# Attention in groups of three heads, four groups in flight, with the experts' weights split inside it

## The reference

```python
def _sot(q):
    qn = q / (norm(q) + 1e-08)
    C = where(eye, 1000.0, 1.0 - einsum('bhnd,bhmd->bhnm', qn, qn))
    log_K, log_v = -C / 0.1, 0
    for _ in range(10):
        log_u = log_marg - logsumexp(log_K + log_v[..., None, :], axis=-1)
        log_v = log_marg - logsumexp(log_K + log_u[..., :, None], axis=-2)
    z = exp(log_u[..., :, None] + log_K + log_v[..., None, :])
    return where(eye, 1.0, z / max(z))
attn = softmax(_sot(q) * 16 ** -0.5)
out = einsum('bhnm,bhmd->bhnd', attn, v)
...
for e in range(8):
    mid = relu(einsum('bsd,fd->bsf', x, W1[e]) + b1[e])
    out = out + w[..., e:e + 1] * (einsum('bsf,df->bsd', mid, W2[e]) + b2[e])
```

## Time and profile before

| | |
|---|---|
| median of 3 runs | 5091.24 us (5083.55 to 5093.23) |
| the profiled execution | 5082.8 us, of which its span 5081.0 us |
| embed and project | 0 to 1203 us |
| attention | 1209 to 3991 us |
| the weights (`prepare`) | 3994 to 4057 us |
| router, experts, combine | 4060 to 5081 us |
| ScalarE busy, whole span | 60% |
| matmuls of `multiply` (L653) | 58368 |

### The profile page before, as it was taken

One profiled execution on the slowest core, in us unless ns is written; L12 is line 12 of the kernel. 1 busy time (PEld: TensorE's weight loads), 2 busy tenths in 40 slices (PEclk: granted clock), 3 DMA queues, 4 the chain that ended last, 5 costly groups with the idle time before them and its releaser, 6 DMA issues. The chain is left out here.

```text
span 5081.0 us, 191812 instructions
## 1 busy us (share of the span) xinstructions
PE 4568.4 (90%) x84561; PEld 3640.2 (72%) x84562; DVE 3744.7 (74%) x8549; ACT 3051.0 (60%) x4474; POOL 310.8 (6%) x349
## 2 busy tenths in 40 slices
PE   5999999885999999999999999999999278599990
PEld 4777777642788888888888888888888144377770
DVE  8999999743577777777777777777777644355557
ACT  4777777633566666666666666666664234377771
POOL 0000000000000000000000000000000014433330
PEclk9999999986999999999999999999999576699995
DMA  1000000032000000000000000000000222322214
GB/s 63 33 35 27 27 27 27 29 98 66 14 16 17 22 16 16 22 17 16 16 23 16 16 21 17 16 16 23 16 12 9 92 89 97 112 69 67 71 60 152
DMA packets 164003, 203.02 MB, mean 40 GB/s; under 512 B 66736, under 2 KB 141744, under 8 KB 160752
## 3 DMA queue, kind: packets, MB, share of 16 engines
q1 hardware_dynamic: 149680, 159.86, 10.5%
q0 software_dynamic: 13632, 32.66, 1.8%
HBM read 123.64 MB, written 68.81 MB: 38 GB/s over the span
## 5 line engine op out<-in xcount | busy, mean ns | idle before, releaser
L653 PE MATMUL y_ps<-k_sb,x_sb 128*12 128x256 f16 x58368 | 1683.4, 273 | 13.3 <-DVE x_sb L890 13.0
L653 PEld LDWEIGHTS y_ps<-k_sb,x_sb 128*12 128x12 bf16 x58368 | 1425.6, 88 | 186.9 <-issue 24.4
L772 ACT ACTIVATE y_sb<-y_ps 128x256 f32<-128x256 f32 x912 | 348.3, 382 | 841.8 <-PE y_ps L653 841.8
L781 ACT ACTIVATE k_new<-cos,k_bias 128x512 f32<-128x512 f32 x768 | 520.9, 683 | 171.2 <-PE cos L680 171.2
L663 PEld LDWEIGHTS turned_x<-rows_in,y_sb 128*128 128x128 f32 x3648 | 477.7, 191 | 118.3 <-issue 71.6
L921 DVE CUSTOM_DVE_ANT_0 plan<-plan,u_rows,v_last 128x512 f32<-128x512 f32 x768 | 535.2, 744 | 4.3 <-issue 0.3
L663 PE MATMUL turned_x<-rows_in,y_sb 128*128 128x16 f32 x3648 | 526.6, 258 | 8.4 <-ACT y_sb L772 8.2
L256 PE MATMUL acc<-w_hl,feat_h 128*128 128x384 f16 x2688 | 454.6, 327 | 87.5 <-ACT feat_h L241 87.5
L795 ACT ACTIVATE plan<-plan,p_bias,p_scale 128x1024 f32<-128x1024 f32 x384 | 464.2, 1238 | 9.7 <-DVE p_scale L932 9.7
L909 DVE TENSOR_TENSOR plan<-k_sb 128x1024 f32<-128x1024 f16 x384 | 459.3, 1217 | 0.0
L936 DVE TENSOR_TENSOR k_sb<-k_new,k_sb 128x2048 f16<-128x2048 f32 x192 | 436.1, 2272 | 30.4 <-ACT k_sb L789 30.4
(11 more groups left out here) (256 smaller groups left out, 7199.3 us busy)
## 6 DMA issues: line engine op xcount, KB each, us to landing
x_in_sb<-expert_rows SPq DMA_DIRECT2D x39, 528.0 KB, 3.7
xt<-in_x_dram SPq DMA_DIRECT2D x16, 1280.0 KB, 5.9
q_left<-q_parts SPq DMA_DIRECT2D x192, 64.0 KB, 3.0
q_right<-q_parts SPq DMA_DIRECT2D x192, 64.0 KB, 3.0
y<-expert_results SPq DMA_DIRECT2D x32, 384.0 KB, 3.7
v_parts<-v_sb SPq DMA_DIRECT2D x16, 408.0 KB, 2.4
v_in_sb<-v_parts SPq DMA_DIRECT2D x48, 136.0 KB, 3.5
h_tokens<-h_sb SPq DMA_DIRECT2D x16, 384.0 KB, 2.5
```

Source lines behind the costliest of these rows:

```text
L653: last = nc.tensor.matmul(y[a][32 * c:32 * c + XW, :, :], high[:, j, XW * h:XW * (h + 1)], k_sb[s][:, h, :, at:at + P], start=(h == 0 and ...
L772: nc.scalar.activation(y_sb[a][:, :, :], y[a][:, :, :], ACT.Copy).then_inc(rows_read[a], 1)
L781: nc.scalar.activation(k_new[h % 2][:, c, :], cos[:, c % 2, :], ACT.Exp, bias=k_bias[:, 0:1], scale=1.0 / (REG * Q_SCALE ** 2), accum_out= ...
```

## The change

The groups have three heads (`GROUP`), so there are 64. A new group starts every five cycles (`APART`), and each takes 19, so up to four are in flight. Groups of the same parity m share one product: `multiply(m, cycle)` does all heads of the two groups g with g % 2 = m in one accumulation over one bank of rows, with a stationary block 18 columns wide, 96 matmuls for six heads. `read_rows`, `turn` and `next_x` are then also one for both groups. K lies in a ring of 16 heads.

Time is counted in points, three to a cycle, and a head follows the one before by five points. What is done for a head at a point counted from its own is given by `BUILD` = -23 and `FIN` = 55, in a function `point(q)` on each engine. As 15 points are one group, what an engine does at a point depends on q modulo 5 (and 15). The orders within a cycle are those at the end of each engine's part below. `start(g)` makes the first vector of group g.

`prepare` is gone. The weights go through attention in 28 pieces of 128 x 768: one is loaded every 15 points and its maximum taken (`largest`), then `scales`, then each is loaded again, split (`high_of` on ScalarE, `low_of` on VectorE) and stored to DRAM by SyncE. `route` loads the stored parts, 9.4 MB, with two DMAs from ScalarE's queue.

```diff
-GH = 4
-GROUPS_PER_IMAGE = HEADS // GH
-ALL_GROUPS = IMAGES * GROUPS_PER_IMAGE
+GROUP = 3
+ALL_HEADS = IMAGES * HEADS
+ALL_GROUPS = ALL_HEADS // GROUP
+PER_IMAGE = HEADS // GROUP
 REG, ITERS = 0.1, 10
-YOUNG, OLD = 9, 10
-CYCLES = 10
-XW = 3 * GH
-XS = XW + 3
+STEPS, APART = 2 * ITERS - 1, 5
+LAST_CYCLE = APART * (ALL_GROUPS - 1) + STEPS - 1
+BUILD, FIN = -23, 55
+FIRST_POINT, LAST_POINT = BUILD, 5 * (ALL_HEADS - 1) + FIN + 12
+K_RING = 16
+XROW, XW, XS = 64, 6 * GROUP, 7 * GROUP
+XSLOT = TB * XROW + 3 * GROUP
+COLS = 2 * TB * GROUP
+PIECE = FFN
+PIECE_OF = [(part, k) for part, pieces in ((0, EXPERTS), (1, EXPERTS), (2, EXPERTS * DIM // P)) for k in range(pieces)]
+PIECES = len(PIECE_OF)
+LARGEST_FROM, MAX_POINT, SPLIT_FROM = 4, 15 * 33 + 1, 34
...
+def head_at(point, offset):
+
+    H, rest = divmod(point - offset, 5)
+    return H if rest == 0 and 0 <= H < ALL_HEADS else None
+
...
+def active(m, cycle):
+
+    return [(g, cycle - APART * g) for g in range(max(m, cycle // APART - 4), min(cycle // APART, ALL_GROUPS - 1) + 1)
+            if g % 2 == m and 0 <= cycle - APART * g < STEPS]
...
+        k_sb = sb("k_sb", [P, K_RING, 2, TB * TOKENS], F16)
+        row_sums = two("row_sums", [P, TB, GROUP], F32)
+        x_sb = two("x_sb", [P, 2 * XSLOT], F32)
...
+        raw, part_h, part_l = two("raw", [P, PIECE], F32), two("part_h", [P, PIECE], F16), two("part_l", [P, PIECE], F16)
...
+            def load_q(g):
+                image, third = g // PER_IMAGE, g % PER_IMAGE * GROUP * HD
+                after(sp, cos_ready, (g - 1) * GROUP * TB)
...
+            for at in range(FIRST_POINT // 15 - 1, LAST_POINT // 15 + 1):
+                for load_or_store, g in ((load_q, at + 2), (load_v, at - 3), (store, at - 5)):
+                    if 0 <= g < ALL_GROUPS:
+                        load_or_store(g)
+                if 0 <= at - SPLIT_FROM - 2 < PIECES:
+                    store_halves(at - SPLIT_FROM - 2)
+                if 0 <= at + 1 - LARGEST_FROM < PIECES:
+                    load_raw(at + 1 - LARGEST_FROM, 0)
+                if 0 <= at + 1 - SPLIT_FROM < PIECES:
+                    load_raw(at + 1 - SPLIT_FROM, 1)
+            for s in range(2):
...
+            def multiply(m, cycle):
+
+                groups = active(m, cycle)
+                if not groups:
+                    return
+                after(pe, x_new[m], step_of(m, cycle))
+                heads = sorted(((g // 2 % 2, h, g) for g, age in groups for h in range(GROUP)))
+                for g, age in groups:
+                    if age == 0:
+                        after(pe, first_x, g + 1)
+                        after(pe, k_built, (g + 1) * GROUP)
+                for e, h, g in heads:
                     for j in range(TB):
+                        window = e * TB * XROW + j * XROW + h * XW
                         for c in range(TB):
                             at = j * TOKENS + c * P
-                            last = nc.tensor.matmul(y[a][32 * c:32 * c + XW, :, :], high[:, j, XW * h:XW * (h + 1)],
-                                                    k_sb[s][:, h, :, at:at + P],
-                                                    start=(h == 0 and j == 0), stop=(h == GH - 1 and j == TB - 1))
-                last.then_inc(product[a], 1)
-
-            def turn(a, n):
...
+            def turn(m, cycle):
+
+                if not active(m, cycle):
+                    return
+                n = step_of(m, cycle)
...
+            def u_to_rows(H):
+                g, h = H // GROUP, H % GROUP
+                after(pe, xt_ready, g + 1)
+                after(pe, scale_ready, H)
...
+            def times_v(H):
+                g, h = H // GROUP, H % GROUP
                 after(pe, p_ready, H * 2 + 2)
...
+            def point(q):
+                for c in range(TB):
+                    H = head_at(q, BUILD + c)
+                    if H is not None:
+                        cosines(H, c)
+                H = head_at(q, FIN + 5)
+                if H is not None:
+                    max_to_rows(H)
+                if q == MAX_POINT:
+                    weight_max_to_rows(head_at(q, FIN + 1))
+                H = head_at(q, FIN + 1)
+                if H is not None:
+                    u_to_rows(H)
+                H = head_at(q, FIN + 9)
+                if H is not None:
+                    times_v(H)
+                H = head_at(q, FIN + 11)
+                if H is not None:
+                    turn_v(H)
+
+            for cycle in range(FIRST_CYCLE, END_CYCLE):
...
+            for cycle in range(FIRST_CYCLE, END_CYCLE):
+                multiply(0, cycle)
+                point(3 * cycle)
+                multiply(1, cycle)
+                for m in range(2):
+                    turn_x(m, cycle)
+                turn(0, cycle)
+                point(3 * cycle + 1)
+                turn(1, cycle)
+                point(3 * cycle + 2)
...
+            def point(q):
+                n, rest = divmod(q - 4, 15)
+                if rest == 0 and 0 <= n - SPLIT_FROM < PIECES:
+                    high_of(n - SPLIT_FROM)
+                H = head_at(q, FIN + 10)
+                if H is not None:
+                    read_v(H)
+                for half in range(2):
+                    H = head_at(q, FIN + 7 + half)
+                    if H is not None:
+                        weights(H, half)
+                for c in range(TB):
+                    H = head_at(q, BUILD + c)
+                    if H is not None:
+                        exponents(H, c)
+                H = head_at(q, BUILD + 4)
+                if H is not None:
+                    high_parts(H)
+
...
+            for cycle in range(FIRST_CYCLE, END_CYCLE):
+                read_rows(0, cycle)
+                point(3 * cycle)
+                read_rows(1, cycle)
+                for m in range(2):
+                    read_xt(m, cycle)
+                point(3 * cycle + 1)
+                point(3 * cycle + 2)
...
+            def next_x(m, cycle):
+                groups = active(m, cycle)
+                if not groups:
+                    return
+                going = sorted(g // 2 % 2 for g, age in groups if age < STEPS - 1)
+                after(dve, turned[m], step_of(m, cycle) + 1)
+                for g, age in groups:
+                    if age == STEPS - 1:
+                        done = nc.vector.reciprocal(v_last[g % 2][:, :, :], tr[m][:, g // 2 % 2])
+                        if not going:
+                            done.then_inc(x_new[m], 1)
+                if going:
+                    slots = slice(going[0], going[-1] + 1)
+                    split(tr[m][:, slots], m, slots, x_steps[m], steps_before(m, cycle), x_new[m])
+
+            def start(g):
+                e = g // 2 % 2
+                after(dve, k_exp, (g + 1) * GROUP * TB)
...
+            def scale_of(H):
+                after(dve, max_rows_ready, H + 1)
...
+            def point(q):
+                n, rest = divmod(q - 1, 15)
+                if rest == 0 and 0 <= n - LARGEST_FROM < PIECES:
+                    largest(n - LARGEST_FROM)
+                if rest == 0 and n == LARGEST_FROM + PIECES:
+                    own_largest()
+                if q == MAX_POINT:
+                    scales()
+                n, rest = divmod(q - 6, 15)
+                if rest == 0 and 0 <= n - SPLIT_FROM < PIECES:
+                    low_of(n - SPLIT_FROM)
+                for half in range(2):
+                    H = head_at(q, FIN + half)
+                    if H is not None:
+                        join(H, half)
+                H = head_at(q, FIN + 5)
+                if H is not None:
+                    scale_of(H)
+                for half in range(2):
+                    H = head_at(q, FIN + 2 + half)
+                    if H is not None:
+                        times_u(H, (2 * half, 2 * half + 1))
+                H = head_at(q, FIN + 12)
+                if H is not None:
+                    normalise(H)
+                H = head_at(q, BUILD + 7)
+                if H is not None:
+                    low_parts(H)
+                if (q + 1) % (3 * APART) == 0 and 0 <= (q + 1) // (3 * APART) < ALL_GROUPS:
+                    start((q + 1) // (3 * APART))
+
+            for cycle in range(FIRST_CYCLE, END_CYCLE):
...
+            for cycle in range(FIRST_CYCLE, END_CYCLE):
+                point(3 * cycle)
+                next_x(0, cycle)
+                point(3 * cycle + 1)
+                next_x(1, cycle)
+                point(3 * cycle + 2)
...
-        prepare(nc, w, keep)
-        route(nc, h, att, ident, w["small"], keep, rows, soft_rows_out)
+        route(nc, h, att, ident, w["small"], keep, halves, rows, soft_rows_out)
...
+            for kept, part in ((keep["w1"], halves[0]), (keep["w2"], halves[1])):
+                nc.scalar.dma_start(kept[:, :, :, :], part).then_inc(halves_in, 16)
```

(39 more changed lines are left out.)

598 lines of the change are left out of this document (207 added, 391 removed).

## The result

The changed kernel takes 5300.5 us (median of 4 runs, 5281.9 to 5312.0) against 5089.0 (5083.6 to 5093.2) for the kernel before: 1.0413 times its time, 95% interval 1.0381 to 1.0445. It is slower, by 211 us; 5260 was forecast, with 5110 to 5360 as the range. The profiled execution has a span of 5280.1 us against 5081.0.

A forecast was written before the change was run, and what follows sets the result against it. TensorE, busy 500 of 500 us in attention, was taken as the bound. From 5082.8 us, +197 attention, -65.5 stage, +5 contention, +32 clock and 0 fill gave 5251; with 8.4 for the median, 5260 us, range 5110 to 5360.

The forecast's parts named there:

- The waits: TensorE idle in attention at group starts, the bank and late ScalarE: 9.85 us over two groups, say 5.0 a group.
- The start of an even group: Before product 0 TensorE waits for start(g), queued behind low_parts on VectorE: 4.2 us idle.
- the third: ScalarE in a group's last cycle makes sums, turn 1 and times_v 1.3 us late every second group, replacing 0.9.
- The work: TensorE's attention work without waits: 39.75 us a group of three, 13.25 a head, with 123 us saved on turns.
- rival E: Wider stationary blocks in the products cost 1 ns more each: 58 us more, 5318 us; chance 0.03.
- The clock: Half rate on TensorE after even starts: 4 us spells, 64 us in all, half taken, +32 us, 0 to 80 kept.
- the second wait: u_to_rows waits for scale_of to read its bank: 1.5 us idle at point 10 modulo 15, 0.55 at 5.
- rival D: Clock falls at every start and stays down longer, or the bank wait drops it too: 5290 to 5360 us; chance 0.11.
- Fill, stage and router: Fill and drain 0 (-15 to +15); stage between attention and router -65.5 us; contention at router's start +5 us.
- B: TensorE stays the bound in attention, VectorE early enough, only the gains stand: 4908 us; chance 0.14.
- C: Only the start of a group is paid, 2.55 us a group: 5071 us; slower from 2.9 us of waits; chance 0.08.
- A: The forecast itself: attention's waits stand in the open as walked, 5260 us, doubt 64 us; chance 0.64.

The follow-up runs named there:

- experiment 1: Changed kernel with the first vector of a group made two points earlier on VectorE; 5174.8 us, 1.0167 of the kernel before.
- experiment 2: Changed kernel with scale_of ahead of join within a point on VectorE; 5178.7 us, 1.0174 of the kernel before.
- experiment 3: Changed kernel with both the earlier first vector and scale_of ahead of join; 4986.4 us, 0.9805 of the kernel before.
- experiment 5: Kernel of experiment 1 with 26 unread matmuls filling the wait for scale_of at point 11 modulo 15; 5082.8 us, 0.9968 of the kernel before.
- experiment 6: Kernel of experiment 3 with the experts' weights as before: stage prepare back, no pieces in attention, no loads of halves; 5056.2 us, 0.9918.
- experiment 7: Kernel of experiment 3 with turn_v ahead of u_to_rows within a point on TensorE; 4966.6 us, 0.9728 of the kernel before.
- experiment 4: Changed kernel with 56 unread matmuls ahead of the wait before product 0 of every even group; 5278.0 us, 1.0373 of the kernel before.

## Why the prediction came out right

Right were the direction, the reason and the size, the last in part because errors cancelled: against the profiled executions the waits were put 56 us too high, the work 64 us too low and the clock at least 42 us too low. Term by term, from these executions:

**The waits: mechanism right, sum 20% too large.** A pair was walked to 9.85 us of idle TensorE and has 8.1. The start of an even group: 4.2 walked, 3.68 measured. The bank at point 10: 1.5, once with 0.25 more, measured 1.56 and 1.61. At point 5: 0.55, measured 0.33 (the 3.8 us of the four waits for p_scale, less these two, by two). The step that failed was the third: ScalarE's lateness was put at 1.3 us in every second group, and the row of pv shows 0.2 in the whole pair; at the odd start, which it was to cover, 0.15 us stands where 0.9 was walked. The list also left out the wait at `scales`, 1.65 us once in the run, since the pieces of the experts' weights were taken to cost TensorE nothing. Experiments 1, 2 and 3 show that it is the order that makes these waits, not VectorE's load: the same work in another order fits under TensorE's.

**The work: undersized by 2 us a pair.** 79.5 us was the sum; experiment 3 has 81.5 busy. The wider blocks are not in it: 96 matmuls of 18 columns take 2.73 us, 28.4 ns each with the step to the next instruction, against 28.1 before, and inside such a stream one follows the other after 26.6 ns, against 26.8 before; so rival E falls. The turns are 0.47 and 0.42 (3947.50 to 3947.97, 3948.24 to 3948.66), as taken. What was missed lies for the most part in `cosines`: one chunk now stands alone at its point and is often followed by something else. It takes 0.28 us with the maximum behind it (3958.99 to 3959.27) but 0.36 with a product behind it (3963.93 to 3964.29), where a chunk in the pairs of before took 0.27; a pair of groups has 24 chunks. Added up over the trace from each start to the next, idle time left out, the 24 chunks of experiment 3's pair take 8.1 us, and as many took 6.8 before (81.2 for 288); that is 1.3 of the 2. Another 0.6 is in the products, 52.0 us for 51.4. The step from the last matmul of a stream to the next instruction is 0.20 us at 128, 96 and 48 matmuls alike, and shorter streams pay it more often.

**The clock: undersized.** Half of 64 us was taken. The product behind the start costs 5.05 - 2.73 = 2.3 us more, in every even start of the regular stretches that was looked at, 32 times about 74. In the other stretch, the five pairs from 2363 to 2834 us take 471 us for 461 regular ones: there spells stand behind the 1.6 us waits too, and the wait at `scales` is in it. The sum weighed the half rate by idle time as a matter of the start alone; that the second wait can drop the clock as well was named only in rival D. Experiment 5 shows that half rate to be worth 101 us where these waits alone are left.

**Fill, stage and router.** 0 was taken for fill and drain. Taking every pair at the steady length, an estimate, 32 x 92.2 = 2950 us of the 3029.4 are pairs; 79 are left where 93 were, -14. The stage gave 63.8 of 65.5. From the router's first load on, 9.8 us were lost for 5. The fourth load, 48.0 us behind the first (51.5 in experiment 3), stands at 43.7 in experiment 6, which has no loads of halves, so that part goes with them. The rest is not shown to be theirs: from its router's first load to its end experiment 6 takes 1055.3 us, where the changed kernel takes 1031.1 and the kernel before 1021.4. The 16.3 us before attention are not shown to come from the change, which touches nothing there, and lie within the spread of these executions: from 1007 to 1050 us the granted clock is 0.50 in the execution of before and 0.81 in that of after, on the same code, and the first matmul of attention comes at 1226.07 in experiment 1, at 1225.20 in experiment 3 and at 1233.83 in experiment 7, against 1231.01 before.

The rivals: B (all waits hidden, 4908 us) did not come, since nothing of start's 4 us vanished; with the waits taken out by hand experiment 7 comes to 4967 us, still above B, which lacks the 2 us of work in each pair. C's point of decision was put at 2.9 us of waits a group, and lies lower, because the work was undersized: experiment 5 has 4.2 us a pair waited or filled (85.7 - 81.5), 2.1 a group, at the full clock, and is level with the kernel before but for 0.3%. The changed kernel, with 4.0 us of idle and 1.2 of half rate a group, is well above that, and experiment 3, with 0.6, below.

Of D more came true than the sum has of it. The clock falls at every start, and in one stretch behind the second wait too; its price, 74 us and more, lies in D's 64 to 130 and not at the 32 of the sum, though in the 0 to 80 kept for the range. But it is back at the next product, and does not stay down as in the earlier trace rows. The measured 5300 us lie in the 5290 to 5360 of D as well as within the 64 us that A was given. The time alone does not tell the two apart; the traces show waits somewhat short of A's with a clock at the low end of D, and that the sum came so near is in part luck.

The signs that were named all came: TensorE at 91% in a window of 500 us, 3.7 us waits of `y_ps` at the even starts, 1.6 us waits of `u_rows` twice in a pair, and 46.1 us a group where 45 was said.

## What to carry to other kernels

When work is laid out as fixed lists, the mean load of an engine says nothing of whether it is in time; walk one period, and ask at each wait how much of the other engine's list stands before the thing that is waited for. What many wait for (a first vector, a read that frees a bank) goes to the front of its slot, long independent work behind it: two such moves of a few lines were worth 6% here. And count a short recurring wait at more than its length where the matmul clock may fall behind it: in experiment 1 each 1.57 us of wait cost another 1.7 in half rate.

## What the runs showed of the hardware

A wait of 1.57 us in TensorE's dense work was followed by 3.4 us at half the clock in experiment 1, where in the changed kernel's regular stretch the same wait was not and the longer one of 3.7 us was. In experiment 4 three of four such waits were followed by a spell. A single wait of 1.65 us, among pairs that ran at 1.00 throughout, was followed by a window of 6.8 us at 0.53 (experiment 3). Waits of 0.47 us (experiment 3) left the clock at 1.00 over 500 us. Filling 1.6 us of idle, twice in a pair, with 26 matmuls that nobody reads made a kernel 2.0% faster. Taking away one kind of wait only moved the fall of the clock to the other, so that the two cures together gave more than their sum. By the Trainium skill (TensorE: Matmul & The Clock Gate, The HAM clock gate) the clock gate stands at half rate by default and activity releases it. Experiments 1 and 5, which differ in whether the wait is idle or busy, agree (0.96 and 1.00 over a pair).
